# Down products of the four-chosen experts: weights held in the array, sums kept by features and turned back per chunk

## The reference, cut to what matters

```python
topk_idx, topk_weight = _gate(x, gate_w, e_bias)          # 4 of 16 experts for each token
g = jnp.einsum('th,eih->eti', x, gate_proj)                # 64 inner features for each expert
u = jnp.einsum('th,eih->eti', x, up_proj)
inter = jax.nn.silu(g) * u
expert_out = jnp.einsum('eti,ehi->eth', inter, down_proj)
y = jnp.einsum('tkh,tk->th', expert_out[topk_idx, jnp.arange(T)[:, None]], topk_weight)
shared_out = jax.nn.silu(hidden_states @ shared_gate_w.T) * (hidden_states @ shared_up_w.T) @ shared_down_w.T
return y + shared_out                                       # added to x
```

## Time and profile before

| | us |
|---|---|
| median of 3 runs | 1594.3 (1593.11 to 1594.4) |
| profiled execution, its time | 1595.39 |
| its span | 1593.6 |
| PE busy | 1485.9 (93%) |
| DVE busy | 1357.6 (85%) |
| ACT busy | 930.5 (58%) |
| POOL busy | 293.7 (18%) |

### The profile page before, as it was taken

How to read it: one execution, slowest core, us unless ns; L and a number is a source line. 1 busy time by engine, 2 the same in 40 slices (tenths; PEclk the granted TensorE clock), 3 DMA queues, 4 the chain that set the end, 5 groups by cost and what they waited for, 6 DMA issues and landing times. The chain is left out here.

```text
span 1593.6 us, 28311 instructions
## 1 busy us (share of the span) xinstructions
PE 1485.9 (93%) x10635; PEld 782.2 (49%) x10635; DVE 1357.6 (85%) x2452; ACT 930.5 (58%) x1755; POOL 293.7 (18%) x350
## 2 busy tenths in 40 slices
PE   8999999999999999899998888877999999989899
PEld 3122222222222222488874333323888877769787
DVE  7999999999999999376667999998776668777686
ACT  3189999999999999633235666754332242222232
POOL 4200000000000000000016878874000110020100
PEclk7599999999999999899999999999999999999899
DMA  3340111000000001000002222220000012300123
GB/s 109 121 143 28 32 35 30 26 25 25 26 25 26 26 25 55 6 1 1 1 2 67 67 66 73 68 66 20 1 1 1 1 32 77 108 1 1 54 86 103
DMA packets 41331, 66.18 MB, mean 42 GB/s; under 512 B 11444, under 2 KB 18661, under 8 KB 40490
## 3 DMA queue, kind: packets, MB, share of 16 engines
q1 hardware_dynamic: 41194, 64.37, 13.4%
HBM read 56.68 MB, written 6.75 MB: 40 GB/s over the span
## 5 line engine op out<-in xcount | busy, mean ns | idle before, releaser
L917 DVE TENSOR_REDUCE row_max<-ps 128x1 f32<-128x1024 f32 x512 | 583.6, 1215 | 11.6 <-PE ps L703 11.4
L823 ACT ACTIVATE probs<-ps 128x512 f32<-128x512 f32 x944 | 506.3, 596 | 52.6 <-PE ps L718 36.2
L703 PE MATMUL ps<-k_stack,q_stack 48*128 48x512 bf16 x1024 | 326.8, 403 | 10.6 <-DVE row_max L917 6.4
L644 PE MATMUL ps<-probs,v_head 128*16 128x256 f32 (+1 forms) x3920 | 316.5, 395 | 1.1 <-issue 1.1
L718 PE MATMUL ps<-q_stack,k_stack 51*128 51x512 bf16 x944 | 287.2, 385 | 0.0
L1542 PE MATMUL ps<-s_hc,ident 128*128 128x512 f32 x256 | 138.5, 626 | 49.0 <-DVE s_hc L1788 44.0
L703 PEld LDWEIGHTS ps<-k_stack,q_stack 48*128 48x128 bf16 x1024 | 59.0, 95 | 249.4 <-DVE row_max L917 221.2
L1114 ACT ACTIVATE x_gate<-ps 128x512 f32<-128x512 f32 x128 | 76.3, 598 | 178.1 <-PE ps L131 178.1
L1490 POOL TENSOR_TENSOR s_dbx<-s_dx,s_b_rows 128x512 f32<-128x512 f32 x128 | 159.5, 1271 | 35.6 <-DVE s_h L1779 35.1
L644 PEld LDWEIGHTS ps<-probs,v_head 128*16 128x16 f32 x3920 | 65.6, 94 | 199.8 <-issue 102.4
L1779 DVE TENSOR_TENSOR_SCAN s_h<-ps,s_state,s_dbx 128x512 f32<-128x512 f32 x128 | 157.0, 1269 | 1.8 <-ACT ps L1673 1.7
(11 more groups left out here) (354 smaller groups left out, 1966.6 us busy)
## 6 DMA issues: line engine op xcount, KB each, us to landing
s_b_rows<-s_b_dram SPq DMA_DIRECT2D x64, 256.0 KB, 3.2
y_spread<-y_probs_dram SPq DMA_DIRECT2D x128, 128.0 KB, 3.0
q_stack<-q_parts_dram SPq DMA_DIRECT2D x30, 96.0 KB
k_stack<-k_parts_dram SPq DMA_DIRECT2D x30, 96.0 KB
w_w<-w_dram SPq DMA_DIRECT2D x1, 2048.0 KB, 7.9
q_stack<-q_parts_dram SPq DMA_DIRECT2D x30, 64.0 KB
k_stack<-k_parts_dram SPq DMA_DIRECT2D x30, 64.0 KB
o_dram<-o_sb SPq DMA_DIRECT2D x60, 32.0 KB
```

The costliest lines, as they stand in the source:

```text
L644: last = nc.tensor.matmul(core.ps[32 * c:32 * c + VROWS, O_BANK, cut], v_head[buf][:, kt, :], probs[:, m % RING, c * CH:(c + 1) * CH][:, cut],
L703: last = nc.tensor.matmul(core.ps[:, 2 * b + r, :], qst[buf][0:KROWS, u * P:(u + 1) * P], kst[buf][0:KROWS, key:key + CH], start=True, sto ...
L823: nc.scalar.activation(probs[:, us % RING, c * CH:(c + 1) * CH], core.ps[:, S_BANK + n % S_RING, :], ACT.Exp).then_inc(exp_done, 1)
L917: nc.vector.tensor_reduce(mx[:, head % 2, u, b:b + 1], core.ps[:, 2 * b:2 * b + 2, :], mybir.AxisListType.XY, ALU.max).then_inc(max_done, 1)
```

## The change

The down product of a unit becomes one matmul: the down matrix of the pair is the weight in the array and the 512 tokens of `hidden` move. The result has features on the partitions and 512 tokens along the bank, and accumulates in `DOWN` as before. At a chunk's end ACT copies the bank to a new SBUF tile `sumT` (`copy_sum`), PE turns it in four 128 by 128 transposes back into `DOWN` (`turn_sum`), and DVE's `add` waits for the turned sums. On PE, at unit 0 of chunks 1 to 3, `up(g+3)` and then `turn_sum` of the chunk before are put ahead of `down(g)`. On ACT `copy_sum` of the chunk before stands at unit 0, behind `silu` and `copy_probs`, and so ahead of `silu`, `copy_turned` and `tanh` of units 1 and 2. Both also stand once behind the last unit.

```diff
+    sum_copied = core.sem(f"{tag}_sum_copied")
+    sum_turned = core.sem(f"{tag}_sum_turned")
+    sumT = sb("sumT", [P, CH])
 ...
-        for k in range(TPC):
-            weight = w["w_down1"][:, u - 1, :] if u else w["sh_down"][:]
-            last = nc.tensor.matmul(core.ps[:, DOWN, k * P:(k + 1) * P],
-                                    hidden[g % SETS][0:rows_of(u), k * P:(k + 1) * P], weight,
-                                    start=u == 0 and k == 0,
-                                    stop=u == UNITS - 1 and k == TPC - 1)
-        last.then_inc(down_done, 1)
+        weight = w["w_down1"][:, u - 1, :] if u else w["sh_down"][:]
+        nc.tensor.matmul(core.ps[:, DOWN, :], weight, hidden[g % SETS][0:rows_of(u), :],
+                         start=u == 0, stop=u == UNITS - 1).then_inc(down_done, 1)
+
+    def turn_sum(pe, c):
+        pe.wait_ge(sum_copied, c + 1)
+        for k in range(TPC):
+            last = nc.tensor.transpose(core.ps[:, DOWN, k * P:(k + 1) * P], sumT[:, k * P:(k + 1) * P], core.ident[:])
+        last.then_inc(sum_turned, 1)
+
+    def copy_sum(act, c):
+        act.wait_ge(down_done, (c + 1) * UNITS)
+        if c:
+            act.wait_ge(sum_turned, c)
+        nc.scalar.copy(sumT[:], core.ps[:, DOWN, :]).then_inc(sum_copied, 1)
 ...
     def add(dve, c):
-        dve.wait_ge(down_done, (c + 1) * UNITS)
+        dve.wait_ge(sum_turned, c + 1)
 ...
+                if u == 0 and c:
+                    up(pe, g + SETS)
+                    turn_sum(pe, c - 1)
                 down(pe, g)
-                if g + SETS < LAST:
+                if g + SETS < LAST and not (u == 0 and c):
                     up(pe, g + SETS)
+            turn_sum(pe, NC_ - 1)
             if following:
                 core.keep_busy(0, 10)
 ...
                 if u == 0 and c:
                     copy_probs(act, c)
+                    copy_sum(act, c - 1)
 ...
+            copy_sum(act, NC_ - 1)
```

## The result

The changed kernel takes 1616.66 us (median of 4 runs, 1614.92 to 1617.88), the kernel before 1594.35 beside it: a ratio of 1.0145, interval 1.0132 to 1.0157, so 22.3 us slower. The forecast was 1613.4, 3.3 us less. The profiled execution of the changed kernel took 1615.54 us with a span of 1613.8; before it was 1595.39 and 1593.6. Of all runs in this document one, of `both_orders`, took 3467.71 us, where the six others of that kernel took 1597.9 to 1600.1; the comparisons leave it out.

The account below looks back on a forecast made before the run. DVE was taken to bind units 1 to 5, PE the later ones, with engine order deciding the turns. 14.7 + 2.6 + 2.8 - 1.0 = 19.1 us on 1594.3 gave 1613.4, range 1606 to 1621.

Parts of the forecast that it names:

- The regimes: Inside a chunk: DVE binds units 1 to 5 at 2.70 us each, PE from there to unit 8.
- near no change: Rival: delays as computed, but DVE and PE win nearly all back inside a chunk; chance 0.03.
- The down products: Two passes of 0.43 us replace eight; 0.03 less in each of 34 PE-bound units, 1.0 us gained.
- The rival in which the loads set the price: Each down pass costs its 0.11 us load, saving 0.43 a unit over 72 units: 1583 us; chance 0.02.
- The turn into chunks 1 and 2: Four turns: ACT's queue delays cut and score, then up and transposes delay add; 14.7 us lost together.
- The small loss of 2.7 at the first turn of `y1`: Turn into chunk 1: DVE already waited there for the spread's DMA, now hidden, so only 2.7 us lost.
- The queue on ACT: copy_sum delays ACT's copies, cut and score; rival: absorbed, 1.8 us less at four turns, 1606 us; chance 0.08.
- The ends: At each stage's end, copy and transposes lie bare: 1.4 us each, 2.8 together.
- the estimate for an idle PE's first load: At a stage's end, 0.1 us for the first load before the transposes, within the 1.4.
- The clock: Rival at the turns: PE's clock falls, 3 to 4 us each, 3 to 14 more, 1617 to 1627; chance 0.08.
- a fall of the clock other than at the openings: Sign of a wrong prediction: the clock drops in the two stages other than at their openings.
- The place on which the doubt rested: Opening of `y1`: PE mostly waited and turned single tiles, granted clock 0.57 over 1293 to 1295.

Follow-up runs that it names:

- both_orders: Changed kernel with copy_sum moved behind copy_turned on ACT and up(c,3) behind down(c,0) on PE; 1598.9 us, ratio 1.0029.
- warm: Changed kernel plus six dummy f32 matmuls on PE ahead of score at the turns into chunks 1 and 2; 1612.67 us, ratio 1.0121.
- act_order: Changed kernel with copy_sum moved behind silu and copy_turned of unit 1 on ACT; 1605.29 us, ratio 1.0071.
- pe_order: Changed kernel with up(c,3) put back behind down(c,0) on PE, so turn_sum follows score at once; 1614.52 us, ratio 1.0130.
- down_only: Kernel before with only the new down product, its sums not turned back; 1591.7 us, ratio 0.9991.
- turn_aside: Kernel before with new down in chunks 0 to 2, copy behind copy_turned, transposes into another bank at unit 2, add at unit 3; 1596.59 us, ratio 1.0017.
- add_aside_old: Kernel before with its old down; for chunks 0 to 2 ScalarE copies the bank and GpSimd adds it to the residual instead of DVE; 1593.24 us, ratio 1.0001.
- add_aside_new: turn_aside with ScalarE copying the turned sums at unit 3 and GpSimd doing the add instead of DVE; 1594.61 us, ratio 1.0011.
- turn_only: Changed kernel with the old down product of eight passes, copy, transposes and both orders kept; 1615.92 us, ratio 1.0139.
- pe_order_warm: pe_order plus six dummy f32 matmuls on PE ahead of score at the turns into chunks 1 and 2; 1607.76 us, ratio 1.0087.

## Why the prediction was right, and where it was off

**The regimes.** Units 1 to 5 keep the pace of 2.70 on DVE (in chunk 1 of `y2` L2221 of unit 1 starts at 1541.19 and that of unit 5 at 1551.99, 10.80 us for four units against 10.81 in the earlier trace rows), and nothing of a late turn is won back inside a chunk. The rival "near no change" falls with it.

**The down products.** Two passes are 0.43 apart, as taken from the earlier trace rows, in 28 of the 72 units, among them those at the end of `y2`, and mostly 0.5 in the others, never closer; a PE-bound unit fell from 2.27 to 2.25. The term was -1.0 and measured -0.7. The rival in which the loads set the price, 0.43 a unit, falls.

The Trainium skill ("TensorE: Matmul & The Clock Gate", "Back-to-back issue gap") gives 81 ns and 131 ns for a load and matmul of 128 and 512 columns, by which, as an estimate, a `down` would be 0.39 us cheaper. The trace shows 0.02 for these f32 operands, and the measurement decides.

**The turn into chunks 1 and 2.** The chain of steps holds. From t0 = 1533.90 (1532.88 + 1.02) the rows above give `copy_sum` at t0 + 0.05, L242 at 1.48, the cut at 2.13, `score`'s first pass at 2.97 (its load predicted at 2.84), the transposes at 5.33 to 5.93 (to 5.78), `add` at 5.97 (5.82) and L2221 at 7.29 (7.15). The 0.14 too little is mostly `score`'s start behind the cut: 0.15 from the cut's end at 1536.72 to the first pass, where the prediction had 0.04 to the first load. The PE gaps that were named are there, 1.59 before `score` (1.6) and 0.87 behind the transposes (0.8). Without falls of the clock (`warm`) the six turns cost 17.2 where 17.3 was computed. The small loss of 2.7 at the first turn of `y1` rests on a row in which the store was slow; the changed kernel hides that wait, as the prediction says, but the wait itself was a matter of that execution.

**The queue on ACT.** That it is not absorbed was right; `act_order` puts 1.8 on it at each turn, the number of the rival.

**The ends.** 1.29 and 1.24 instead of 1.4 each: the transposes come 0.04 behind the copy's end, with no 0.1 more (1609.03 + 0.59 = 1609.62, first pass at 1609.66), and the estimate for an idle PE's first load was not needed.

**The clock.** This is the term that was missed. The prediction gave it a chance of 0.08 as a rival, with 3 to 4 us for each fall, and took it out of the sum on the ground that PE runs an `up` and soon a `down` at each turn. It did fall at two of four turns in the profiled execution, for 2.9 us together, and without it (`warm`) the kernel is some 4 us faster. With 2.9 on the forecast it would have been 1616.3. The prediction itself named a fall of the clock other than at the openings as a sign of being wrong, and by that sign this step was wrong; the total came close because two falls cost only 2.9. Their price was put too high for this kernel (2.2 and 0.7), as the clock comes back after 3.4 to 10.2 us in these traces; their likelihood was put too low.

The place on which the doubt rested was the right one to read, but its row shows PE busy for 1.75 of the 2 us. The waiting that the prediction speaks of lies just ahead of it (timeline of PE, kernel before):

```profile
1291.08 1.01 PE L232 MATMUL ps<-ident,xn 128*128 128x128 f32 x4 [0.78 <-DVE xn L223]
1293.25 1.87 PE L2135 MATMUL ps<-w_gate,xnT 128*128 128x16 f32 x8 [1.16 <-ACT xnT L242]
```

The clock fell there at 1293.3, as `score` began behind waits of 0.78 and 1.16 us. At the turns the change brought a wait of 1.6 us ahead of the same `score`. So the trace before held a case for a higher chance. `pe_order` speaks for the other half of the argument, that the `up` between `score` and the transposes, 1.4 us dear on the path, holds the clock up at some turns: without it all four fell.

What stays open: why the same instructions lose the clock at 1338 and 1566 and not at 1366 and 1538. No run here separates that. The 2.2 us that came back ahead of `y2` weren't tested by a run of their own, but the twelve traces order that stretch by the clock: it takes 88.7 us where the clock is at 0.50 for 10.2 us of it, 87.1 to 87.9 at 6.8 us, and 86.3 to 86.6 at 3.4 us.

## What to carry to other kernels

Where an engine's order is written by hand, a new instruction costs what stands behind it in that queue: here one copy of 0.6 us that had itself to wait for the last `down`, put ahead of three operations that others waited for, cost 1.8 us four times over. Put the copy behind them, and read at each wait on TensorE whether the granted clock holds around it. Before a difference between two traces is put down to a change, compare the clock and the transfers in the parts that the change doesn't touch. A shorter instruction gains only in the units its engine binds, and a step moved off a turn where its engine waits anyway to a place where it is the bound turns from nearly free to its full price.

## What the hardware showed that was not expected

TensorE's clock fell though the engine was never idle for longer than 1.6 us at a turn. By kernel, falls at the four turns into chunks 1 and 2, counted in windows of 2 us:

| | PE waits before `score` | between `score` and the transposes | falls |
|---|---|---|---|
| before, `down_only`, `turn_aside`, `add_aside_old`, `add_aside_new` | no | (no transposes at the turn) | 0 |
| `act_order` | no | `up` | 0 |
| `both_orders` | no | nothing | 1 |
| changed kernel | 1.6 us | `up` | 2 |
| `turn_only` | 1.6 us | `up` | 1 |
| `pe_order` | 1.6 us | nothing | 4 |
| `pe_order_warm` | dummies, then 0.24 us | nothing | 2 |
| `warm` | dummies, then 0.24 us | `up` | 0 |

In these traces the dummies in the wait and the `up` behind `score` each go with fewer falls, and both together with none. A count is from one trace: `turn_only` has the waits of the changed kernel and one fall fewer. The mean granted clock of the whole program in the four executions of each kernel agrees with the larger differences: 0.960 to 0.961 for `pe_order`, 0.964 to 0.965 for the changed kernel, 0.967 to 0.969 for `pe_order_warm`, 0.968 to 0.969 for `warm` and `act_order`; for `turn_only` it is 0.965 to 0.970.

GpSimd's add of two SBUF operands slowed DVE's operations of the same kind, while a multiply that reads one operand from PSUM kept its 0.69 beside it. L2297 took 0.60 us instead of 0.22 in all four chunks where it met the add in `add_aside_new`, and each time ended 0.08 us behind the add. A multiply with both inputs in SBUF took twice its 0.69 beside the last of these adds:

```profile
1578.25 1.29 POOL L2214 TENSOR_TENSOR x_res<-x_res,y_sums 128x512 f32<-128x512 f32 x1 [21.36 <-ACT y_sums L2209]
...
1578.71 1.38 DVE L2246 TENSOR_TENSOR y_gate<-y_gate,y_spread 128x512 f32<-128x512 f32 x1 [1.28 <-ACT y_gate L2228]
```

The Trainium skill ("GPSIMD Engine Reference", "1. Specifications") says that the two engines share their SBUF interfaces and that DVE instructions with two SBUF inputs contend for them; the trace agrees, with 0.4 us for each of the four short operations and 0.7 for the long one.
